# Self-attention of a decoder layer: the second slot of a group's split keys and values filled by transfers

## What is computed

```python
def _L0_attn_ref(x, freqs_cos, freqs_sin, wq, wk, wv, wo, k_cache, v_cache, block_idx):
    DIM, NH, NKV, HD = (512, 32, 8, 128)
    BLOCK, NBLK, TOPK = (32, 128, 16)
    n_rep = NH // NKV
    q = (x @ wq.T).reshape(b, l, NH, HD)
    k = (x @ wk.T).reshape(b, l, NKV, HD)
    v = (x @ wv.T).reshape(b, l, NKV, HD)
    q, k = apply_rope(q, ...), apply_rope(k, ...)
    k_sel = k_cache[block_idx].reshape(-1, NKV, HD)      # 16 blocks of 32 positions
    v_sel = v_cache[block_idx].reshape(-1, NKV, HD)
    k_full = jnp.concatenate([k_sel, k[0]], axis=0)      # 512 + 128 = 640 keys per group
    v_full = jnp.concatenate([v_sel, v[0]], axis=0)
    ...repeat each of the 8 groups for its 4 heads...
    scores = jnp.einsum('bhld,bhtd->bhlt', qh, k_full) / math.sqrt(HD)
    attn = jax.nn.softmax(scores, axis=-1)
    out = jnp.einsum('bhlt,bhtd->bhld', attn, v_full)
    return out.transpose(0, 2, 1, 3).reshape(b, l, NH * HD) @ wo.T
```

## Time and profile before

| what | value |
|---|---|
| median of 3 runs | 1940.7 us (1939.71 to 1942.23) |
| the profiled execution | 1942.56 us, its span 1940.8 us |
| self-attention, units 2 to 57 | 73 to 782 us of the span |
| TensorE busy, granted clock over the span | 97%, 0.993 |
| VectorE, ScalarE, GpSimd busy | 69%, 53%, 50% |

### The profile page before, as it was taken

How to read it: one execution, slowest core, us unless ns; L and a number is a source line. 1 busy time by engine, 2 the same in 40 slices (tenths; PEclk the granted TensorE clock), 3 DMA queues, 4 the chain that set the end, 5 groups by cost and what they waited for, 6 DMA issues and landing times.

```text
span 1940.8 us, 31760 instructions
## 1 busy us (share of the span) xinstructions
PE 1890.5 (97%) x10146; PEld 1625.5 (84%) x10146; DVE 1347.5 (69%) x2177; ACT 1030.7 (53%) x2265; POOL 963.3 (50%) x771
## 2 busy tenths in 40 slices
PE   8899999999999999998999999999999999999998
PEld 6788888888888888876888888888888888888887
DVE  7788888888888888867666666666667666667132
ACT  4666666666666666655444444444444444446444
POOL 3777777777777777772332332323233223214643
PEclk9999999999999999998999999999999999999999
DMA  7555444445445444551111111011111011002232
GB/s 253 129 126 123 122 122 122 120 122 122 123 124 123 122 121 121 153 136 50 47 34 41 46 46 46 24 39 46 46 46 46 28 46 46 25 23 87 92 115 80
DMA packets 98361, 169.03 MB, mean 87 GB/s; under 512 B 24834, under 2 KB 31106, under 8 KB 97794
## 3 DMA queue, kind: packets, MB, share of 16 engines
q1 hardware_dynamic: 98306, 168.33, 31.9%
HBM read 82.26 MB, written 2.10 MB: 43 GB/s over the span
## 4 chain that ended last, share of the span: by engine, by line
PE 80%; DVE 10%; issue 5%; ACT 3%; SPq 1%; POOL 0%; DMA 0%; DVEq 0%; ACTq 0%
PE bank L1329 22%; PE bank L1330 21%; PE bank L1331 21%; PE bank L1409 7%; DVE negmax L959 4%; DVE xacc L978 2%; PE bank L1552 2%; PE bank L1553 2%; PE bank L1597 2%; PE bank L1598 2%; PE bank L1607 1%; DVE probT L967 1%; ACT prob L610 1%; DVE oT_lo L972 1%; PE bank L1399 1%
## 5 line engine op out<-in xcount | busy, mean ns | idle before, releaser
L460 POOL TENSOR_TENSOR pT_lo<-pT_lo,pT_hi 128x512 fp32r<-128x512 f32 x320 | 407.4, 1297 | 190.2 <-ACT pT_hi L551 190.2
L978 DVE SCALAR_TENSOR_TENSOR xacc<-bank,rinv,xacc 128x512 f32<-128x512 f32 x504 | 363.8, 733 | 5.0 <-PE bank L1331 5.0
L610 ACT ACTIVATE prob<-bank,negmax 128x640 f32<-128x640 f32 x256 | 203.8, 796 | 273.0 <-DVE negmax L959 272.6
L967 DVE STREAM_TRANSPOSE probT<-prob 128x640 f32<-128x640 f32 x256 | 214.4, 838 | 82.4 <-ACT prob L610 82.3
L959 DVE TENSOR_REDUCE negmax<-bank 128x1 f32<-128x640 f32 x256 | 206.8, 808 | 21.1 <-PE bank L1409 14.9
L443 POOL TENSOR_TENSOR xwo_lo<-xwo_raw,xwo_hi 128x512 fp32r<-128x512 f32 x32 | 41.4, 1292 | 332.7 <-ACT xwo_hi L551 332.7
L551 ACT ACTIVATE pT_hi<-pT_lo 128x512 fp32r<-128x512 f32 x320 | 185.8, 622 | 7.3 <-DMA pT_lo<-probT 7.3
L443 POOL TENSOR_TENSOR xwq_lo<-xwq_raw,xwq_hi 128x512 fp32r<-128x512 f32 x32 | 41.4, 1293 | 285.2 <-ACT xwq_hi L551 285.2
L719 ACT ACTIVATE xprob<-xscore,negmax 128x128 f32<-128x128 f32 x256 | 99.5, 392 | 91.9 <-DVE negmax L1151 91.9
L1329 PE MATMUL bank<-wx_hi,cT_hi 128*128 128x256 f32 x512 | 142.1, 278 | 1.1 <-DVE xk L1087 1.1
L1331 PE MATMUL bank<-wx_hi,cT_lo 128*128 128x256 f32 x512 | 141.9, 277 | 0.0
(11 more groups left out here) (197 smaller groups left out, 5591.5 us busy)
## 6 DMA issues: line engine op xcount, KB each, us to landing
pT_lo<-probT SPq DMA_DIRECT2D x1024, 80.0 KB, 2.1
w_raw<-in_w SPq DMA_DIRECT2D x64, 256.0 KB, 2.8
wx_raw<-in_wq SPq DMA_DIRECT2D x32, 256.0 KB, 2.7
wo_raw<-in_wo SPq DMA_DIRECT2D x32, 256.0 KB, 2.7
wx_raw<-in_xwv SPq DMA_DIRECT2D x16, 512.0 KB, 3.2
xwk_raw<-in_xwk SPq DMA_DIRECT2D x32, 256.0 KB, 3.2
xwq_raw<-in_xwq SPq DMA_DIRECT2D x32, 256.0 KB, 3.1
xwo_raw<-in_xwo SPq DMA_DIRECT2D x32, 256.0 KB, 2.6
```

The lines of the kernel that those rows point to most:

```text
L460: g.tensor_tensor(tile, tile.bitcast(F32), four(pT_hi[:, j, :]), ALU.subtract).then_inc(a["pTlo"], 1)
L610: s.activation(prob[:, i % 2, :].rearrange("p (a t) -> p a t", a=2), S_bank[i % 2], ACT.Exp, bias=negmax[:, u % 2, i:i + 1], scale=1.0, ac ...
L967: v.transpose(probT[:, u % 2, :, :, i * 32:(i + 1) * 32], prob[:, i % 2, :].rearrange("p (t j n) -> p j t n", j=4, n=32)).then_inc(a["turn ...
L978: v.scalar_tensor_tensor(xacc[:, 4 * half + i, :], M, rinv[:, k, i:i + 1], xacc[:, 4 * half + i, :], ALU.mult, ALU.add).then_inc(sems["y"], 1)
```

## The change

The 16 splits into slot 1 are gone from ScalarE and VectorE. SyncE copies slot 0 to slot 1 instead: in step u = 2 of each group, after the 16 transfers of the unit and before the weight load, four transfers of 320 KB (128 partitions of 2560 bytes), `K_hi` and `K_lo` with a semaphore of their own and then `V_hi` and `V_lo` with another. TensorE waits for the keys' copies in front of the scores of step u = 3 and for the values' in front of the first product of unit 4. The splits of the next group into slot 0 stay with ScalarE at the ends of u = 5 and u = 7, behind a wait for the copies of the present group; those of VectorE go to steps u = 6 and u = 8 and stand there between the third `turn` and the accumulation, ahead of the fourth maximum. `c_first` waits for the values' copies too.

```diff
+            def a_copy(it, u):
+                if u % 8 == 2:
+                    sp.wait_ge(a["Klo"], it + 1)
+                    for z in (K_hi, K_lo):
+                        sp.dma_start(z[:, 1].bitcast(F32), z[:, 0].bitcast(F32)).then_inc(s_kcopy, 16)
+                    sp.wait_ge(a["Vlo"], it + 1)
+                    for z in (V_hi, V_lo):
+                        sp.dma_start(z[:, 1].bitcast(F32), z[:, 0].bitcast(F32)).then_inc(s_vcopy, 16)
...
                 if n == UNITS - 6:
-                    sp.wait_ge(a["Vlo"], NH // 2)
+                    sp.wait_ge(a["Vlo"], NKV)
+                    sp.wait_ge(s_vcopy, 32 * NKV)
...
                     a_turn(it * 8 + u, it, u)
+                    a_copy(it, u)
                     a_load(it, u)
...
# ScalarE, end of the step
-                if u % 2 == 1 and (not static or n // 4 + 1 < UNITS // 4):
-                    pair_ = (it + (u // 4 + 1) // 2, (u // 4 + 1) % 2)
-                    last_ = static and n // 4 + 2 == UNITS // 4
-                    if u % 4 == 1:
-                        k_group(*pair_)
-                    if u % 4 == (1 if last_ else 3):
-                        v_group(*pair_)
+                if u == 5 and (not static or n < UNITS - 8):
+                    act.wait_ge(s_kcopy, 32 * (it + 1))
+                    k_group(it + 1, 0)
+                if u == 7 and (not static or n < UNITS - 8):
+                    act.wait_ge(s_vcopy, 32 * (it + 1))
+                    v_group(it + 1, 0)
...
# VectorE
                 if more1:
                     turn(n + 1, it, u + 1, 2)
+                if u == 6 and (not static or n <= UNITS - 8):
+                    dve.wait_ge(s_kcopy, 32 * (it + 1))
+                    k_group(it + 1, 0, it + 2)
+                if u == 8 and (not static or n <= UNITS - 8):
+                    dve.wait_ge(s_vcopy, 32 * (it + 1))
+                    v_group(it + 1, 0, it + 2)
                 if outs:
                     add(2, 1)
                 if more1:
                     maxes(n + 1, 1 - k, 3)
-                if u % 2 == 1 and (not static or n // 4 + 1 < UNITS // 4):
-                    pair_ = (it + (u // 4 + 1) // 2, (u // 4 + 1) % 2, it * 2 + u // 4 + 2)
...
# TensorE
-                    if u % 4 == 0:
-                        pe.wait_ge(a["Vlo"], it * 2 + u // 4 + 1)
+                    if u == 0:
+                        pe.wait_ge(a["Vlo"], it + 1)
+                    if u == 4:
+                        pe.wait_ge(s_vcopy, 32 * (it + 1))
...
-                            if u % 4 == 3:
-                                pe.wait_ge(a["Klo"], it * 2 + u // 4 + 2)
+                            if u == 3:
+                                pe.wait_ge(s_kcopy, 32 * (it + 1))
+                            if u == 7:
+                                pe.wait_ge(a["Klo"], it + 2)
```

More of the change, by code:

```diff
@@ L174, in decoder_layer @@
             "pThi", "pTlo", "pv", "oThi", "oTlo", "q", "qhi", "qlo", "rinv", "wo", "y")}
+        s_kcopy, s_vcopy = sem("K_copied"), sem("V_copied")
         s_pT = [sem(f"pT_in{i}") for i in range(2)]
@@ L317, in _ @@
                 a_turn(u, 0, u)
+                a_copy(0, u)
                 a_load(0, u)
@@ L328, in _ @@
                 a_turn(56 + u, 7, u)
+                a_copy(7, u)
                 a_load(7, u)
```

## The result

The changed kernel takes **1948.7 us**, median of six runs (1944.28 to 1951.35); the kernel before, run beside it on the same chip, takes 1940.49 (1939.36 to 1943.98, six runs). The ratio is 1.0034, with a 95% interval of 1.0022 to 1.0045: slower by 6.6 us, at least 4.3 and at most 8.7 (the two medians themselves lie 8.2 apart, inside this interval). The forecast was 1942.1 with its own range to 1947, and "no change" as the likeliest sign; the time lies above that and inside the full range of 1928 to 1951.

A forecast was written before the change was run, and what follows sets the result against it. TensorE, busy 97% of the span, bounds the kernel, so only its stalls count. Removed splits -26.5, low halves +14.6, copies +12.8, end of stage +0.5 sum to +1.4: 1942.1 us, own range 1938 to 1947, full range 1928 to 1951.

The forecast's parts named there:

- "no change": Whole kernel: time within 0.2% (3.9 us) of the kernel before, chance 0.49; slower 0.30, faster 0.21.
- Removed, 26.5: Self-attention: TensorE's stalls behind the 30 splits at ends of odd steps all go, 26.5 us saved.
- the first split: Start-up: the first split shows no separable stall, so its removal saves zero, at most 0.8 us.
- Low halves, 14.6: Even steps: GpSimd's wx_lo holds VectorE's moved K_lo or V_lo; 1.04 us of stall, 14 times, 14.6 us.
- The 0.65 of absorbed lateness: Unit steps: of VectorE's 1.49 us lateness TensorE loses 0.84; 0.65 is absorbed, and subtracted from the low halves' 1.69.
- Copies, 12.8: Start of step 3: TensorE waits for K's copies, issued behind SyncE's 16 transfers; 12.8 us over 8 groups.
- the rival of 1950.1: Slow copies: SBUF to SBUF copies run at the transposing transfers' rate, wait 2.6 x 8 = 20.8 us; chance 0.24.
- no clock is charged: Copy waits: 1.6 us idle is little over a 1.24 stall that kept the clock at 1.00, so no cost.
- 1.6 us, 8 times: Step 3 of each group: TensorE's wait, with K_lo landing 3.5 us after K_hi's issue; lower bound 1.3, upper 2.6.
- the 2.0 from which the prediction called itself wrong: Profile after: TensorE's wait for K's copies near 1.6 us, 8 times; wrong from 2.0 on, or if absent.
- the sum: Whole kernel: -26.5 + 14.6 + 12.8 + 0.5 = +1.4 us, so the median becomes 1942.1.
- End of the stage, 0.5: Unit 59: its transfers start 4 to 5 us later behind V's copies; cost 0.5 us, bounds 0 and 3.

The follow-up runs named there:

- Both cures: Changed kernel with K's copies in step 1 and VectorE's low halves ahead of the second transposition: 1915.98 us; with V's copies in step 1 too, 1915.49.
- The cut-down GpSimd: Changed kernel with GpSimd's wx_lo and wo_lo in steps 6 and 8 covering only 1/32 of their columns: 1933.13 us, ratio 0.9958.
- the empty place: Changed kernel with K_lo and V_lo moved from behind the third transposition to ahead of the second, where GpSimd is idle: 1931.16 us, ratio 0.9936.
- the two repetitions: The changed kernel, unaltered, profiled a second and a third time: 1946.41 and 1949.96 us.
- Only the first group's keys early: Changed kernel with the first group's keys alone copied in step 1, groups 1 to 7 still in step 2: 1942.65 us, ratio 1.0006.

## Why the prediction was right or wrong

- *Removed, 26.5:* right. Both cures together give 26 to 27. Of the first split I had said "zero, at most 0.8"; unit 2 came 1.5 sooner in this pair of profiles. That this is the split isn't shown: between three executions of the changed kernel alone the same mark moves from 71.71 to 74.40, to both sides of the 73.17 of before.
- *Low halves, 14.6:* right in what holds VectorE and in size (15.3, 1.09 each for 1.04), wrong in the way by which it reaches TensorE. Held to GpSimd's end, done 0.68 after it, the next one stretched: each as read in the earlier trace rows. The cut-down GpSimd and the empty place show the cause twice over. I looked for the stall in front of the next step's output projection, by way of oT_lo; it comes within the same step, by way of the accumulation that frees the bank. The 0.65 of absorbed lateness was read on the way of oT_lo. That the size came out all the same is partly luck. On the way of the accumulation the room happens to be similar: in the kernel before the accumulation of the earlier trace rows ends at 310.88, 0.87 ahead of the output projection at 311.75, so 1.70 - 0.87 = 0.83 are left, and the rest of the 1.09 is an estimate of what the restart costs. The Trainium skill, "SBUF — State Buffer", section Who interferes with whom, calls the port pair that VectorE and GpSimd share an exclusive lock. The trace agrees: K_lo takes 1.77 beside wx_lo, and 0.81 and 0.78 where GpSimd is idle or soon done.
- *Copies, 12.8:* right in mechanism, and in size for the steady groups: 1.6 forecast, 1.53 to 1.62 found. Copies as slow as the transposing transfers, the rival of 1950.1, is out: K_lo landed 3.4 after K_hi's issue, not 4.5. The median came close to that rival's time by coincidence. The Trainium skill, "SBUF — State Buffer", section Door 1: The DMA port swizzle, says that 32 partitions reach 8 of the 16 ports and 128 reach all. The trace agrees: with the copies on the queue it moved 1.33 MB in 4 us at a share of 92.0%, 361 GB/s at full share, where the prediction had worked out 239 from the 32-partition transfers.
- **The step that failed** is "no clock is charged", with "1.6 us, 8 times" under it. I took the queue of one steady step (in group 2) for that of all eight groups. In group 0 SyncE has issued without a pause since the start-up, don't show that, and the wait is 2.1 to 3.0 in the profiles with the copies of the change; that is above the 2.0 from which the prediction called itself wrong. And I let one stall of 1.24 behind which the clock held speak for all stalls up to 1.6. The two first groups cost 3.97 + 3.61 where 3.2 was put down: +4.4, of which 1.3 is longer waits and 3.1 the clock (+2.4 and +3.9 in the two repetitions). "Only the first group's keys early" shows the remainder: with waits near 1.6 and no fall the sum holds to 1 us.
- *End of the stage, 0.5:* 0.6, and 0.9 and 1.1 in the two repetitions, within its bounds. In the three kernels in which the keys' copies cost no wait but V's stay in step 2, step 60 is 14.2 to 14.8 long, 1.2 to 1.8 over that of before.
- That the kernel came out clearly slower, and not within what can be told from no change, followed from that one step: +1.4 and +4.4 make 5.8, against 6.6 (4.3 to 8.7) measured. In the profiled execution the low halves add 0.7 to this and the start-up takes 1.5 away, which leaves the 5.1 of the table.

**What stays open:** from what length of a wait on the clock falls. Between 1.8 and 3.0 it fell mostly but not always (it held once at 1.79, a length at which it fell in another execution, and once at 2.89), so something besides the length decides there. Open too is why SyncE's 16 issues in group 1 take 10.03 in some executions and 10.46 or 10.95 in others, and with them the wait 1.36, 1.79 or 2.28.

## What to carry to other kernels

Put a VectorE instruction that takes two SBUF operands where GpSimd is between instructions: the same subtraction cost TensorE a tenth of a microsecond or a whole one here, by its neighbour. Before a transfer goes onto a queue, count the issues ahead of it (16 are 10 us here) in the first round as well as in a steady one, since the queue may still carry a backlog from the start-up; if it is late, look whether it can go a step earlier, where it cost no wait here. Both faults hid a gain of 1.4% that the idea of the change had in it: when a sum comes out at zero, look at each of its costs for a place where it isn't paid.

## What was not expected of the hardware

- A copy of 320 KB from SBUF to SBUF over 128 partitions lands 2.5 us after its issue, one issued right behind it 2.8 after its own, the fourth 3.5: the first two are no slower than the 256 KB loads from HBM (2.7 and 2.9).
- The clock fell behind eight of ten waits of 1.8 to 3.0 us in a stream that is otherwise busy 97%, and a fall cost 1.6 us there (up to 2.9 behind waits over 3.1): two such waits turned "no change" into "slower".
- Of the 16 issues in a row on SyncE's queue in group 1, which take 10.03 us together in some executions, the fifteenth took 1.02 or 1.51 us instead of 0.59 in others, and TensorE's wait for the copies behind them was longer by as much.
